# Chunk attention: value matmuls of two key tiles issued together

## The reference, cut to what matters

```
b, s, d = x.shape                       # 16, 512, 128
Q = (x @ Wq.T).reshape(H, b, s, dkh)    # H = 16, dkh = 8; K and V likewise
scores = einsum('hbqd,hbkd->hbqk', Q, K)
atten = softmax(scores, axis=-1)
out = einsum('hbqk,hbkd->hbqd', atten, V).reshape(b, s, -1)
y = out + x                             # then normalised over each sequence
```

## Time and profile before

| | |
|---|---|
| median of 3 runs | 4069.43 us (4066.49 to 4075.25) |
| the profiled execution | 4086.11 us, its span 4084.4 us |
| TensorE matmul busy | 3511.8 us, 86% of the span |
| VectorE busy | 2711.9 us, 66% |
| ScalarE busy | 2281.1 us, 56% |
| GpSimd busy | 2061.4 us, 50% |
| chunk attention, steps 4 to 36 | from 82 to 872 us of the span |

### The profile page before, as it was taken

How to read it: one execution, slowest core, us unless ns; L and a number is a source line. 1 busy time by engine, 2 the same in 40 slices (tenths; PEclk the granted TensorE clock), 3 DMA queues, 4 the chain that set the end, 5 groups by cost and what they waited for, 6 DMA issues and landing times. The chain is left out here.

```text
span 4084.4 us, 88921 instructions
## 1 busy us (share of the span) xinstructions
PE 3511.8 (86%) x30527; PEld 2149.4 (53%) x30527; DVE 2711.9 (66%) x7206; ACT 2281.1 (56%) x5536; POOL 2061.4 (50%) x2119
## 2 busy tenths in 40 slices
PE   5999999966768999999999999975947775987668
PEld 1333333325754555555555655554936564675446
DVE  6888888855445777777777777754556664655465
ACT  2777777743324666666666666642435552674367
POOL 3333333227436776777677777756421111665175
PEclk9999999975888999999999999965979897897879
DMA  5433333311561212112121212122632222120001
GB/s 101 61 60 60 60 60 60 59 29 59 173 185 42 53 44 51 47 48 50 45 53 43 52 46 49 49 62 86 202 98 65 63 69 49 25 63 6 1 1 43
DMA packets 418240, 252.22 MB, mean 62 GB/s; under 512 B 251186, under 2 KB 344354, under 8 KB 416642
## 3 DMA queue, kind: packets, MB, share of 16 engines
q1 hardware_dynamic: 409156, 228.56, 24.0%
q0 software_dynamic: 8640, 17.97, 1.3%
HBM read 75.12 MB, written 41.75 MB: 29 GB/s over the span
## 5 line engine op out<-in xcount | busy, mean ns | idle before, releaser
L2498 POOL TENSOR_TENSOR ra_prob<-ra_prob,ra_inverse 128x256 f32<-128x256 f32 (+3 forms) x512 | 630.7, 1253 | 386.9 <-DVE ra_inverse L2714 386.6
L2312 DVE TENSOR_REDUCE ca_mx<-ca_ps_s 128x2 f32<-128x1024 f32 x512 | 600.7, 1211 | 117.6 <-PE ca_ps_s L2184 117.3
L2643 ACT ACTIVATE ra_prob<-ra_ps_s,ra_low 128x128 f32<-128x128 f32 (+3 forms) x1024 | 533.6, 531 | 237.4 <-DVE ra_low L2694 237.4
L2249 ACT ACTIVATE ca_pT<-ca_ps_p 128x512 f32<-128x512 f32 x1024 | 545.1, 600 | 203.3 <-PE ca_ps_p L2194 201.7
L2694 DVE CUSTOM_DVE_ANT_0 ra_ps_s<-ra_ps_s,ra_mask 128x128 f32<-128x128 f32 (+3 forms) x1024 | 475.2, 516 | 46.6 <-PE ra_ps_s L2591 46.4
L2184 PE MATMUL ca_ps_s<-ca_kst,ca_qst 128*128 128x512 bf16 x1024 | 392.8, 389 | 22.7 <-DVE ca_mx L2312 9.6
L2194 PE MATMUL ca_ps_p<-ca_qst,ca_kst 128*128 128x512 bf16 x1024 | 386.5, 382 | 4.2 <-ACT ca_pT L2249 4.2
L2649 ACT COPY ra_probT<-ra_ps_t 128x512 f32<-128x512 f32 x384 | 227.1, 591 | 278.7 <-PE ra_ps_t L2537 278.7
L2537 PE MATMUL ra_ps_t<-ident,ra_prob 128*128 128x128 f32 x2560 | 377.4, 278 | 5.1 <-POOL ra_prob L2498 1.2
L2537 PEld LDWEIGHTS ra_ps_t<-ident,ra_prob 128*128 128x128 f32 x2560 | 289.3, 141 | 124.3 <-issue 59.7
L2591 PE MATMUL ra_ps_s<-ra_kz,ra_qz 64*128 64x128 f32 (+3 forms) x2048 | 347.3, 457 | 3.7 <-DMA ra_kz<-ra_rot 2.8
(11 more groups left out here) (411 smaller groups left out, 7159.5 us busy)
## 6 DMA issues: line engine op xcount, KB each, us to landing
moe_w_own<-moe_w1T SPq DMA_DIRECT2D x142, 256.0 KB
ra_qz<-ra_rot SPq DMA_DIRECT2D x512, 64.0 KB, 2.0
ra_kz<-ra_rot SPq DMA_DIRECT2D x512, 64.0 KB, 2.0
ca_kst<-ca_bounce SPq DMA_DIRECT2D x256, 64.0 KB
ca_bounce<-ca_thirds SPq DMA_DIRECT2D x192, 64.0 KB, 2.8
ca_qst<-ca_bounce SPq DMA_DIRECT2D x64, 192.0 KB
moe_hs<-moe_rows SPq DMA_DIRECT2D x142, 66.0 KB
moe_raw<-in_L_ffn_W SPq DMA_DIRECT2D x32, 256.0 KB
```

The costliest lines, as they stand in the source:

```text
L2249: nc.scalar.activation(pT[:, (NS * hp + u) % PRING, :], ps_p[n % NP][:], ACT.Exp).then_inc(sg["drained"], 1)
L2312: nc.vector.tensor_reduce(mx[:, hm % 2, 2 * j:2 * j + 2], ps_s[m % 2][:].rearrange("p (b k) -> p b k", b=2), AX.X, ALU.max)\
L2498: nc.gpsimd.tensor_tensor(at, at, inverse[:, n % PROB, 2 * tile:2 * tile + 2].unsqueeze(2).broadcast_to([P, 2, keys]), ALU.mult)\
L2643: nc.scalar.activation(prob[:, n % PROB, tile, head, 0:keys], part(n, tile)[:, head, :], ACT.Exp, bias=low[:, n % PROB, at:at + 1], scale= ...
```

## The change

The eight visits of a step are joined in twos. Visits 0 and 1 now stand together at u = 11, 2 and 3 at u = 19, 4 and 5 at u = 27, and 6 and 7 at u = 3 of the next step. The earlier of each pair thus moves back by four u; the later stays where it was. No instruction is added or removed, and no engine but TensorE has another order.

```diff
                         if u == 3 and hl is not None:
+                            values(6, hl)
                             values(7, hl)
-                        if hp is not None and u % 4 == 3 and u >= 7:
-                            values((u - 7) // 4, hp)
+                        if hp is not None and u % 8 == 3 and u >= 11:
+                            values((u - 11) // 4, hp)
+                            values((u - 11) // 4 + 1, hp)
```

## The result

| | before | changed |
|---|---|---|
| median | 4074.61 us (4066.49 to 4081.39, 6 runs) | 4104.3 us (4102.41 to 4108.14, 6 runs) |
| span of the profiled execution | 4084.4 us | 4100.7 us |

The ratio is 1.0076, 95% interval 1.0063 to 1.0089: the changed kernel is slower by 0.76%, 29.7 us between the medians. The three more runs of before lie higher than those shown ahead of the prediction (4069.43), so 4104.3 beside the predicted 4103.8 is closer than the prediction was good: forecast were +34.4 us, measured +29.7.

What follows compares the result with a forecast made beforehand. TensorE sets the pace with VectorE not far behind; full steps +28.0, steps 32 and 33 +3.4, steps 34 and 35 +3.0 make +34.4 us on 4069.43, so 4103.8 us, range 4088 to 4119.

Steps and rivals of the forecast that it cites:

- The two stalls: Joined stretch: third and fourth pairs' first scores wait for VectorE's reductions, 0.40 and 0.26 us, 0.66 together.
- The saving of a join: TensorE's second visit follows at once, costing 0.91 us: 0.19 us saved per join, 0.77 a step.
- By stretch: Four stretches of a full step, forecast longer by 0.27, 0.14, 0.38 and 0.21 us; +1.00 a step.
- At ScalarE's pace: Steps 34 and 35, where ScalarE's exponentials set the pace: +0.43 us for each of 7 joins, +3.0.
- Steps 32 and 33: Steps with nothing between scores and visits: 7 joined stretches at +0.48 us each, +3.4.
- (a): Rival: TensorE stays the bound, VectorE keeps up, the join only saves; -38 us, 4032; chance 0.04.
- 0.7 us of cover: Full steps: the eighth shifted score's exponential is done at 3.00, the score due at 3.70, so ScalarE stays covered.
- (b): Rival: stalls come smaller, with reductions 0.12 us shorter each; +8 us at most, 4069 to 4077; chance 0.04.
- (c): Rival: the second visit waits on its own semaphore, costing 1.10 us, not 0.91; +24 on top, 4128; chance 0.07.

Runs made afterwards that it cites:

- e1: The kernel before (separate visits) with VectorE's maximum taken over the first 256 of 512 keys; ratio to before 0.9965.
- e2: The changed kernel (joined visits) with VectorE's maximum taken over the first 256 of 512 keys; ratio to before 0.9933.
- e3: The changed kernel with the projection to V at u = 31 instead of u = 30; ratio to before 1.0043.
- e7: The changed kernel with V's projection at u = 31 from half-sequence 4 on and the norm's statistics at j = 14, a step earlier; ratio to before 1.0043.

## Why the prediction was right

**The two stalls** in a joined stretch were the heart of it, and they came where and as long as forecast: scores 2.35 us after TensorE's return, 0.40 and 0.26 of waiting (0.40 and 0.15 with the maxima's transpose in between). e1 and e2 show that they hang on the length of the reduction, e3 on when it can begin, e7 that the norm has no part in it. That two double banks are what makes them long is argued from the kernel's waits: no run varied the number of banks.

**The saving of a join** was the term that was mis-sized: 0.24 us and not 0.19. The joined visits take 1.86 us, not 1.91; both halves of the second visit follow after 0.43, where I had used the first distance, 0.45, for each. 119 joins at TensorE's pace x 0.05 = 6.0 us, so that the forecast of +34.4 would have been +28.4; the change made 28.0 of the stage. The stage's whole +30.2 and the plain runs' +29.7 are closer to the forecast only because the filling, with the same code, took 2.2 us longer in the profile, and that is chance.

**By stretch**, u = 4 to 11 to u = 28 to 3: forecast 6.14, 6.14, 6.36, 7.53; measured 6.09, 6.10, 6.31, 7.49. Every one is shorter than forecast by 0.04 or 0.05. At ScalarE's pace the four joins from step 34 to 35 made 19.39 us (835.21 to 854.60) into 21.06 (862.48 to 883.54): +1.7 forecast, +1.7 measured. Steps 32 and 33 gave +2.6 of their +3.4.

**The rivals.** (a), TensorE stays the bound, falls; but its condition was tested, and there something that the prediction had not foreseen came up. It said that ScalarE had 0.7 us of cover, which was right with VectorE's stalls in the stretch and gone without them. Even with short reductions the join itself gave 0.49 us a step, where (a) counts 0.77 for it. (b) would have needed reductions that end 0.12 us sooner; they were as long as before. (c), a second visit that starts badly, was wrong in direction.

The Trainium skill has a rule for either side, both in TensorEngine Tiling (Array Packing). The one in Key Properties, on the drain at a change of mode, agrees with the 0.24 us of a join. The one in PSUM Bottleneck, that tiling doesn't speed the emptying of PSUM, agrees with the 0.66 us of stalls in so far as the reductions stayed at 1.21 us; neither says that bunching the tiled matmuls makes the stalls, and these decided.

## What to carry to other kernels

Joining two short visits of an engine saves its switches, but makes one long stretch in which its consumers get nothing, followed by one in which they get too much. In this kernel two buffers store two of the consumer's units of work; if the joined visit and the burst behind it are longer than these, the consumer's idle time before the burst comes back as stalls in it, though on average the consumer is far from full. The sum is short: the time at which the consumer is done with the first item after the visit, plus one consumer's step for each further one, against the producer's own pace. And relieving the consumer of other work helps only where that work delays an item, not where it stands in the idle time. Once the first consumer is quick enough, the next one (ScalarE here, 72% busy) can be the limit of a stretch.

## What the runs showed of the hardware

- A half visit, four instructions on f32 tiles of 128x512, follows the one before it after 0.45 us at first and then every 0.43, through a change of weights, a change of visit and a satisfied wait on a semaphore. Only the entry from bf16 matmuls on the full array (0.31 against 0.215) and the way out (0.12: 1.00 against 0.88) cost. A projection in column groups behind a visit is entered without the way out.
- Not every row of the form 128*32 has that entry. The maxima's transpose starts 0.23 after the score before it (401.01 to 401.24), and the shifted score behind it 0.11 later.
- VectorE's maximum over a double bank is 1.21 us for 1024 columns and 0.69 for 512, so some 0.17 us of it don't depend on the size, if it grows evenly between the two.
- A joined stretch repeats within 0.01 us from step to step (one of over 100 was 0.03 longer), and a sum made by hand from such a timeline was right to 0.05 us per stretch.
